# The first products of an FP4 layer: low-rank pairs in front, their sums a step later, products one step sooner in TensorE's queue

## The reference, cut to what matters

```python
xq = nvfp4_qdq(x2[:, up_reorder_index], SEL_UP)      # FP4 rounding, blocks of 16, last 128 channels kept
wg = nvfp4_qdq(w_gate[:, up_reorder_index], SEL_UP)
wu = nvfp4_qdq(w_up[:, up_reorder_index], SEL_UP)
h = silu(xq @ wg.T) * (xq @ wu.T)                    # hidden width 1376
hq = nvfp4_qdq(h[:, down_reorder_index], SEL_DOWN)
out = hq @ wd.T * mlp_output_scale
out = out + x2 @ lr_A @ lr_B                         # low-rank term, rank 64
x = x + out
```

## Time and profile before

| | |
|---|---|
| median of 3 runs | 870.35 us (869.67 to 870.58) |
| profiled execution | 869.45 us |
| its span, first to last instruction | 868.1 us |
| mean granted TensorE clock | 0.927 of full |
| PE busy | 731.8 us (84%) |
| PE weight loads busy | 543.5 us (63%) |
| DVE busy | 584.3 us (67%) |
| ACT busy | 430.0 us (50%) |
| POOL busy | 191.1 us (22%) |

### The profile page before, as it was taken

One profiled execution on the slowest core, in us unless ns is written; L12 is line 12 of the kernel. 1 busy time (PEld: TensorE's weight loads), 2 busy tenths in 40 slices (PEclk: granted clock), 3 DMA queues, 4 the chain that ended last, 5 costly groups with the idle time before them and its releaser, 6 DMA issues.

```text
span 868.1 us, 11246 instructions
## 1 busy us (share of the span) xinstructions
PE 731.8 (84%) x4112; PEld 543.5 (63%) x4112; DVE 584.3 (67%) x1107; ACT 430.0 (50%) x549; POOL 191.1 (22%) x176
## 2 busy tenths in 40 slices
PE   1787654988999999989979998786779799968998
PEld 1564321656767667666757776564557588966887
DVE  4899977553688879798898863773333332557873
ACT  3756665555776877787756211442212111224452
POOL 0223000022253443454563432021001200000000
PEclk9999965999999999999999998897688899997999
DMA  7644678765375775667753012011001211200000
GB/s 279 203 138 167 209 220 275 236 220 178 124 233 190 225 246 189 221 206 245 214 155 115 37 46 61 17 46 48 1 0 32 62 35 36 66 18 12 25 25 37
DMA packets 56039, 110.55 MB, mean 127 GB/s; under 512 B 9888, under 2 KB 20800, under 8 KB 55984
## 3 DMA queue, kind: packets, MB, share of 16 engines
q1 hardware_dynamic: 42560, 78.43, 27.8%
q10 hardware_dynamic: 9040, 17.30, 6.1%
q0 software_dynamic: 4384, 14.09, 5.8%
HBM read 91.65 MB, written 18.15 MB: 126 GB/s over the span
## 4 chain that ended last, share of the span: by engine, by line
PE 50%; DVE 29%; issue 7%; ACT 6%; DMA 6%; SPq 1%; ACTq 0%; DVEq 0%
PE bank L1108 13%; PE bank L1109 13%; PE bank L1110 13%; DVE hot L1749 3%; PE bank L1396 2%; PE bank L1215 2%; DVE bank L1775 2%; DMA wide_buf<-in_down_flat 2%; ACT hot L1503 2%; DVE x L1872 2%; PE bank L1228 1%; DVE gm L1791 1%; DVE q_a L1822 1%; DMA codes<-c 1%; DVE q_r L1816 1%
## 5 line engine op out<-in xcount | busy, mean ns | idle before, releaser
L1503 ACT ACTIVATE hot<-rep,levels 128x2048 f16<-128x2048 f16 x96 | 193.6, 2056 | 23.1 <-ACT c L1466 10.7
L1108 PE MATMUL bank<-zt_h,w_h 128*128 128x512 f32 (+1 forms) x232 | 92.7, 400 | 2.6 <-DVE zt_l L1860 2.0
L1110 PE MATMUL bank<-zt_h,w_l 128*128 128x512 f32 (+1 forms) x232 | 90.7, 391 | 0.0
L1109 PE MATMUL bank<-zt_l,w_h 128*128 128x512 f32 (+1 forms) x232 | 90.5, 390 | 0.0
L1108 PE MATMUL bank<-w_h,xq_h 128*128 128x512 f32 (+1 forms) x192 | 78.3, 408 | 12.4 <-ACT hid L1602 6.5
L1215 PE MATMUL bank<-hot,diag 128*32 128x512 f16 x1160 | 78.9, 398 | 8.3 <-DVE hot L1749 5.6
L1109 PE MATMUL bank<-w_l,xq_h 128*128 128x512 f32 (+1 forms) x192 | 75.7, 394 | 0.0
L1110 PE MATMUL bank<-w_h,xq_l 128*128 128x512 f32 (+1 forms) x192 | 75.2, 392 | 0.0
L2015 POOL TENSOR_TENSOR q_a<-q_a,q_m 128x384 f32<-128x384 f32 (+3 forms) x34 | 35.7, 1050 | 107.1 <-DVE q_m L1643 107.0
L1215 PEld LDWEIGHTS bank<-hot,diag 128*32 128x32 f16 x1160 | 26.2, 98 | 51.7 <-issue 25.2
L1108 PE MATMUL bank<-w_h,at_h 128*128 128x512 f32 x112 | 49.0, 437 | 6.6 <-DVE x L1872 3.8
(11 more groups left out here) (219 smaller groups left out, 1670.1 us busy)
## 6 DMA issues: line engine op xcount, KB each, us to landing
rep<-codes SPq DMA_DIRECT2D x58, 512.0 KB, 4.7
codes<-c SPq DMA_DIRECT2D x29, 256.0 KB, 3.8
raw<-in_codes_gu_t ACTq DMA_DIRECT2D x14, 512.0 KB, 4.9
sc<-in_scales_gu_t SPq DMA_DIRECT2D x56, 128.0 KB, 4.4
raw<-in_codes_attn_t ACTq DMA_DIRECT2D x8, 512.0 KB, 4.2
raw<-in_codes_down_t ACTq DMA_DIRECT2D x7, 512.0 KB, 6.3
sc<-in_scales_down_t SPq DMA_DIRECT2D x28, 128.0 KB, 3.0
wide_buf<-in_gate_flat SPq DMA_DIRECT2D x5, 512.0 KB, 4.3
```

What stands on the lines that cost most here:

```text
L1108: PE.matmul(psum, lh, rh, start=first, stop=False, **kw)
L1109: PE.matmul(psum, lh, rl, start=False, stop=False, **kw)
L1110: return PE.matmul(psum, ll, rh, start=False, stop=last, **kw)
L1503: S.activation(hots[plan.slot[hot_ring(t), (t, m)]][:], codes_in_place(t), ACT.Relu, bias=bias, scale=slope).then_inc(sem("ramp_act"), 1)
```

## The change

Three orders of steps change; no instruction is added or removed. `low_take` of half 0 goes into `greatest_of_all`, in front of `floor`; that of half 1 goes to step 2. A low-rank step is now: the two `low_add` of the pair before, then the two `low_b` of the next pair. It comes in front of `hmm` in steps 3 to 7 (pairs 0 and 1 in step 3, the last two adds in step 7), and `hmm` of tile s - 2 instead of s - 3 stands in step s, from step 2 on. The four gathers of the next chunk's rows are issued in step 3, and its row turns stay in steps 7 to 10: one in step 7 and two in each later step.

```diff
         p.add("allcol", what)
+        if what == "x":
+            p.add("low_take", 0)
         p.add("floor", what)
...
     def low_rank():
-        for half in range(2):
-            p.add("low_take", half)
+
+        p.add("low_take", 1)
+        yield
+        for n in range(0, NT + 2, 2):
+            for m in range(n - 2, n):
+                if m >= 0:
+                    p.add("low_add", m)
+            for m in range(n, min(n + 2, NT)):
+                p.add("low_b", m)
+                main4(("lb", m), ("dve", "low_add", m))
             yield
-        due = None
-        for n in range(NT):
-            p.add("low_b", n)
-            main4(("lb", n), ("dve", "low_add", n))
-            if due is not None:
-                p.add("low_add", due)
-            due = n
-            yield
-        p.add("low_add", due)
...
     first_hidden, low, second = hidden(0), low_rank(), fetch_pair(1)
-    low_left = NT + 2
     for step, _ in enumerate(turned_tiles([("x", n, 0) for n in range(NT)])):
-        if step >= 3:
-            next(first_hidden)
-        for _ in range(2 if step >= 3 else step > 0):
-            if low_left:
-                next(low)
-                low_left -= 1
-            else:
-                drain(low)
-                next(second, None)
+        if step >= 2:
+            next(low, None)
+            next(first_hidden, None)
+        if step == 3 or step >= 7:
+            next(second)
+        if step >= 8:
+            next(second)
     drain(first_hidden)
```

## The result

The changed kernel takes 839.9 us (median of 4 runs, 838.59 to 842.19) against 870.47 us before (the median of four runs beside it; 870.35 was that of the three shown ahead of the prediction): a ratio of 0.9649, 95% interval 0.9623 to 0.9676. 841.2 us had been forecast. The profiled execution took 842.19 us with a span of 840.8, the slowest of its four; the one before took 869.45.

What follows compares the result with a forecast made beforehand. The prediction took a ring of waits, not any engine's amount of work, as the bound. Next products 31.1 us sooner, less 1.9 for clock, gave 29.2 off 870.35: 841.2 us, range 838.0 to 847.0.

Steps and rivals of the forecast that it cites:

- a ring in series: First products of the FP4 layer: TensorE's products, the add, VectorE's rounding, the turn, each waiting for the one before; step 14.0 us.
- The period: One step of the first products: 7.94 us against 14.0, from products, `low`, turn issue and low-rank pair.
- The cover: Turn issue and low-rank pair, 1.93 us, hide ScalarE's take and Silu, 1.87 us; it fits by 0.06 us.
- Rival C: The 0.06 us of cover fails, ScalarE's `take` and `hfin` stay exposed in three steps: up to 845.0 us; chance 0.13.
- The start: First products at 588.7 instead of 596.27; `low_take` 0 in front of `floor` delays the first rounding by 0.30 us.
- The table load: In step 3, `hfin` 0 includes a 1.28 us load, leaving a gap of 1.4 us before P_1, paid once.
- The tail: From P_7's end to the next products: 8.6 us instead of 7.40, two more splits in front, last gather covered.
- The stage at full clock: Products after P_7 start at 657.6 against 688.66, 31.1 us sooner at a full clock throughout.
- The clock: The level may fall at the start and at the gap in step 3: 1.9 us lost, bounds 0 and 4.
- B: Rival: the clock falls in every step, four more cold stretches of 1.8 us: 848.4 us; chance 0.12.
- D: Rival: the step stays at 14 us, TensorE still waits for VectorE at the turn, only the early start counts: 864; chance 0.03.
- E: Rival: slower, the clock stays low from 588.7 to the end of P_7: 885 us; chance 0.02.

Runs made afterwards that it cites:

- c_pair_behind: The changed kernel with the low-rank pair behind the 24 products of its step instead of in front: 849.05 us, ratio 0.9743.
- f_table_early: The changed kernel with one added Silu activation before the first `low_take`, so that the table load happens there: 840.76 us, ratio 0.9658.
- adds-at-once: The changed kernel with each pair of adds right behind its own low-rank pair, not a step later: 845.73 us, run again 843.52 us.
- e_take_as_before: The changed kernel with `low_take` 0 back in step 1, behind the first turn: 844.49 us, ratio 0.9717.
- h_rows_sooner: The changed kernel with the row turns of chunk 1 one step sooner: 840.06 us, ratio 0.9637.
- g_rec_last: The changed kernel with `hpart` and `rec` of chunk 0 behind the last two row splits: 839.14 us, ratio 0.9666.
- i_fill: The changed kernel with nine extra products that nobody reads, in the two gaps of the start: 839.74 us, ratio 0.9654.
- d_not_sooner: The changed kernel with products of tile s-3 in step s instead of s-2, as before the change: 847.9 us, ratio 0.9756.
- a_late_adds: The kernel before with one edit, each low-rank add two tiles late: 853.38 us, ratio 0.9791.

## Why the prediction was right

- *What bounds the stage.* Right: a ring in series. One edit that cuts it took the period from 14.0 to 9.6 us with the same work on every engine. What the prediction didn't work out is how much of a step is idle time and how much clock: of the 4.35 us that this edit takes from a step, 1.7 are idle time and 2.6 are clock.
- *The period.* 7.94 us forecast, 8.04 measured: a turn in front of the pair costs 0.53 instead of 0.35, `low` 0.23 instead of 0.32. VectorE fits under it, and its delay of the adds turned out not to be needed once the pair is in front. The prediction had credited the late adds with it and hadn't asked what each of the two edits does alone.
- *The cover.* The prediction's 0.06 us were 0.20. From the turn's start to the products it is 609.25 - 607.13 = 2.12 us of cover. The chain on ScalarE takes 608.91 - 607.13 = 1.78 us and 0.14 more until TensorE starts; the 0.14 is read where TensorE does wait for Silu, in c_pair_behind (Silu from 607.55 to 608.17, products at 608.31). Rival C is out for this kernel; c_pair_behind shows what it would have cost.
- *The start.* A to P_0: 588.7 - 577.3 = 11.4 forecast, 11.6 measured, 11.26 where the clock stays up. `low_take` in front of `floor` delays the first turn by 0.14 us, not 0.30 (8.46 us from A before, 8.60 after), and its old place costs 2.3.
- *The table load.* The gap in front of P_1 is 1.14 us, 1.4 had been forecast. ScalarE's row of the load is 1.28 us here as in the earlier trace rows, and Silu follows it at once: 598.94 after 597.64 on the path of the changed kernel, 581.13 after 579.84 in f_table_early. So the 2.66 us that the Trainium skill states in "ScalarE: Activation LUTs", section "What ACT_TABLE_LOAD costs", don't show on this path.
- *The tail.* P_7 to N: 657.6 - 643.3 = 14.3 forecast, 14.18 measured, 1.1 more than before. The last gather was hidden as forecast: the splits behind `rec` ended later; with `rec` moved it is what shows.
- *The stage at full clock.* 111.36 - 31.1 = 80.3 us forecast; the profiles without a fall show 80.40, 80.41 and 80.42.
- *The clock.* The term that was mis-sized for the profiled execution: 1.9 us forecast, 84.53 - 80.40 = 4.1 measured, just past the bound of 4. It fell at both places named: P_0 starts at the lower level, and again P_1. Over the runs it is a term that comes and goes: two profiles of the changed kernel have both falls, while the adds-at-once kernel, whose start is the same, has none in two. Both of those were the fastest run of their group (835.28 and 837.24 us), and the others of that kernel took 842.85 us or more, so nothing shows that the edit keeps the clock up.
- *Rivals B, D, E.* B is out: in steps 4 to 6 the clock is 1.00 in every profile without waits in them. The swing that the Trainium skill describes in "TensorE: Matmul & The Clock Gate", section "A second HAM failure mode: psum-queue depth-cycling", needs small idle times between the groups of products. The full stretch of the earlier trace rows has none, so it couldn't speak against the page. The kernel before does bear the page out: with 1.78 and 1.27 us of idle time in a step its level alternates, in the columns of the earlier trace rows:

```profile
637.40:644.20 6.80, 5.41 (x14) 4.17 (x15) 2.04 (x4) 1.08 (x2) 0.00 (x0) 0.50 0.00 0
644.30:651.00 6.70, 5.41 (x22) 3.64 (x20) 2.31 (x5) 1.19 (x3) 0.00 (x0) 1.00 0.00 0
```

The changed kernel goes through the same banks in 608 to 622 without idle time and stays at 1.00. D and E are out by the period and the clock of the first table.
- *The time.* 841.2 forecast, 839.9 and, in another group of runs, 844.4. The second is 3.2 us above the forecast and within the range; a clock term of 4 instead of 1.9 would account for 2 of it. For the profiled execution 840.3 had been forecast and 842.19 was measured; there the clock term is 2.2 us short (4.1 against 1.9), and the rest of the sum fits within 0.3. That the first median came within 1.3 us is in part luck, as the same kernel gave 844.4 in another group.

## What to carry to other kernels

When all engines are half idle in a stage, look for an instruction that waits for the bottleneck engine and has the next step's preparation queued behind it. Move that one waiting instruction, or move what it waits for ahead of the long work. Its worth is not the length of its own wait (6.83 us here) but the idle time of the bottleneck engine (1.7 us a step) and the clock that came back with it (2.6 us a step). Then check every other kind of instruction for the same pattern before filling the freed place: the row splits made the ring again at once. Where totals scatter by more than an edit is worth, measure the stage between two events in the trace.

## What was not expected of the hardware

- The granted clock falls in some executions and not in others at the same gap. In nine profiles TensorE idles 1.13 or 1.14 us in front of P_1. Four of them fall behind it (both of the changed kernel, e_take_as_before, h_rows_sooner), and all four had also fallen at the start. The four that hadn't fallen at the start (both of adds at once, g_rec_last, i_fill) didn't fall here either. d_not_sooner had fallen at the start, was at the upper level from 602.1 and stayed there. So the two falls aren't independent, and what decides the first stays open. In the changed kernel the clock is 0.58 in the 4 us behind the gap; in i_fill P_1 to P_4 lasts 24.11 us, which is full speed. In a_late_adds two gaps of 1.32 us left the level at 1.00; behind the third, at 638.46, it fell (the first product takes 0.75 against 0.47 us).
- With the clock equal the stage repeats closely: 80.40 and 80.41 us in two profiles of one kernel, taken in different groups of runs, 84.53 and 84.47 in two of another. The two profiled executions of the changed kernel, 842.19 and 845.36 us, differ ahead of the stage: the first `low_a` came at 576.6 us in one and 579.9 in the other, and the lag arises between 136 and 187 us of the span. What causes it was not looked into, and the runs without a profile can't be split in this way.
